# First layer of a four-part transformer kernel: the f16 operand copies move from VectorE to GpSimd

## The chip, the cores and the metric

The kernel runs on one core of one Trainium2 chip. The metric is device microseconds (us) of one execution, the median of several runs. The core has five engines with queues of their own: PE (TensorE, with its weight loads as PEld), DVE (VectorE), ACT (ScalarE), POOL (GpSimd) and SP (SyncE, which only issues DMAs here). They meet only through semaphores.

## What is computed

Eight sequences (B = 8) of 256 tokens with 512 features go through two gated layers. Each adds an attention and a feed-forward part to x:

```python
x = x + tanh(g_xattn[0]) * causal_attention(layernorm(x), ctx, ctx)     # 16 heads of 32, no projections
x = x + tanh(g_ffn[0])   * experts(layernorm(x))                        # 32 experts of 192, 8 per token
x = x + tanh(g_xattn[1]) * projected_attention(layernorm(x), ctx)       # w_q, w_k_img, w_v_img, w_o
x = x + tanh(g_ffn[1])   * ternary_linear(layernorm(x))
```

In the first attention the query is the normalised input, and key and value are both the context. Products need nearly f32 accuracy, so each operand is split into two f16 parts: hi = f16(scale * v), lo = f16(scale * v - hi).

## The kernel before

The program has three stages, each a block with one instruction stream per engine: `layer0` (first attention, gate and sending of rows to expert slots; about the first 330 us), `experts` (160 tiles of 128 rows through the expert weights), and `layer1`. Only `layer0` and, in three lines, `experts` are touched.

**Staging of layer 0.** A batch is one sequence. Its attention has 16 steps (STEPS): 8 for the first half of the queries (keys 0 to 127), 8 for the second half (256 keys), two heads each. In a step PE makes scores (L240, with the causal mask L243), DVE takes their maximum (L325) and scales it to a bias (L327), ACT takes the exponential (L293), PE turns the probabilities (L278), ACT copies them out of PSUM (L305) and PE multiplies them with the context (L258). While batch n runs through its 16 steps, every engine also does the preparation of batch n + 1 (PREP0) and the rest of batch n - 1 (POST0). Which piece is done behind which step is written out by hand in the tables PREP0 and POST0: engine, step number, names of pieces. Within an engine everything runs in that order. Batch 0 has its preparation ahead of the first step, in the order of ORDER_PREP0; the bodies of batches 0 to 6 hold the other seven.

**Preparation pieces.** "ln": DVE takes mean and variance of x (L615, L619, L621), POOL makes the reciprocal root (L605). "c": the two 128-row tiles of the context are split. ACT writes hi (L349), DVE writes lo (L355) and then copies both parts beside themselves in the same `parts` tile (L361), so that each head has four blocks of 32 columns: hi, hi, lo, lo for the context, and hi, lo, hi, lo for the input. "xn": DVE normalises x (L625). "q": the same split and copy for the two tiles of the normalised input. "S0" to "S7": PE turns eight heads of `parts` (L372, eight transposes into one PSUM bank), and DVE (L379), or ACT for S1 and S5 (L318), copies the bank into `stack`, from which the scores are made. S0 and S1 belong to the first context tile, S2 and S3 to the second, S4 to S7 to the two input tiles. PE waits for `parts_ready` ahead of each, and for the copy of the piece two before (the two banks alternate).

The part that copies is this, with the arguments cut; `chain.link` marks an instruction on a semaphore of DVE and waits for it on DVE:

```python
def dve_lo(self, dve, b, i, src, scale, chain):
    j = ORDER[i]
    dve.wait_ge(self.hi_ready, 4 * b.n + i + 1)
    chain.link(scalar_tensor_tensor(self.part(j, 1), src, scale, self.part(j, 0), MULT, SUBTRACT))   # L355
    ...
    self.nc.vector.tensor_copy(dup, of).then_inc(self.parts_ready, 1)                                # L361
```

**POOL in layer 0.** Besides L605 and the second reciprocal root L689 it only issues the indirect DMAs that send the rows of batch n - 1 to their expert slots (L699): 16 per batch, one behind each step (from step 10 of batch n to step 9 of the next body), each behind `probs_made` of its step. In a step, the pieces of the tables stand ahead of the send.

**Rest of a batch on DVE (POST0)** beside the steps of the next: L714 to L726 (division by the sums, gate, variance), L729 (normalised rows, then ACT L681 and L685 and PE L655), L733 (lo part of the rows sent), and the choice of the eight experts (L737 to L782).

**Experts.** For each of the 160 tiles PE loads a code from a table into a register (L1335), turns eight pieces of the tile (L1293), multiplies with gate and up weights (L1305, 12 products), turns the hidden values (L1316) and multiplies with the down weights (L1329). DVE loads a code of its own (L1449). SP loads the block number with bounds (L1157: `min_val=0, max_val=NONE`), the other engines without. `over_tiles` (L1099) writes the first five and last three tiles out, and holds the others in a loop of eight tiles per turn.

**Layer 1** uses the same class Attention with `causal=False`.

Of the kernel before, what the change touches and what calls it, by code (L numbers as in the profile page):

```python
# [14 lines left out]
ALU = mybir.AluOpType  # L15
# [6 lines left out]
QT = S // P  # L22
HC = H // P
NH, D = 16, 32
E, FI, TOPK = 32, 192, 8
# [84 lines left out]
def over_batches(first, body, last):  # L110
# [32 lines left out]
    pool={4: ["ln"]},  # L143
# [47 lines left out]
class Attention:  # L191
# [6 lines left out]
    def __init__(self, nc, sb, sem, bank, tag, causal, scale, v, id32, id16, idb, maskb):  # L198
# [13 lines left out]
        self.hi_ready, self.parts_ready = sem(tag + "hi_ready"), sem(tag + "parts_ready")  # L212
        self.stack_ps, self.stack_ready, self.stack_by_act = sem(tag + "stack_ps"), sem(tag + "stack_ready"), sem(tag + "stack_by_act")
# [138 lines left out]
    def dve_lo(self, dve, b, i, src, scale, chain):  # L352
        j = ORDER[i]
        dve.wait_ge(self.hi_ready, 4 * b.n + i + 1)
        chain.link(self.nc.vector.scalar_tensor_tensor(self.part(j, 1), src.rearrange("p (h d) -> p h d", d=D), scale,  # L355
                                                       self.part(j, 0), ALU.mult, ALU.subtract))
        if j < QT:
            dup, of = self.parts[:, j, :, 1:4:2, :], self.parts[:, j, :, 0:4:2, :]
        else:
            dup, of = self.parts[:, j, :, 2:4, :], self.parts[:, j, :, 0:2, :]  # L360
        self.nc.vector.tensor_copy(dup, of).then_inc(self.parts_ready, 1)  # L361

# [141 lines left out]
def layer0(nc, shared, plan, proj, x, ctx, g_xattn, g_ffn, gate_w, w_experts, mats, ternary):  # L504

    es = ExitStack()
    with es:
# [94 lines left out]
        def pool_prep0(pool, b, piece):  # L602
            if piece == "ln":
                pool.wait_ge(x_var, b.n + 1)
                nc.gpsimd.tensor_tensor(rstd[:, 0, :], mv[:, 0, :, 1], neghalf[:, 0:QT], ALU.pow).then_inc(x_rstd, 1)  # L605

        K_PREP0 = 2 * QT + 2 * QT
# [503 lines left out]
def experts(nc, shared, plan, proj, w_experts, mats, ternary, ctx, vecs):  # L1111

    es = ExitStack()
    with es:
# [4 lines left out]
        def sem(name):  # L1119
            return es.enter_context(nc.semaphore(name))  # L1120
# [161 lines left out]
        def _(pe):  # L1282
# [51 lines left out]
            def step(t):  # L1334
                code = pe.value_load(t_pe[0:1, t.column()])  # L1335
                e, before = code & (E - 1), code >> 5
                if t.at(1).exists():
                    turn(t.at(1))
                gate_up(t, e)
                if t.at(-2).exists():  # L1340
                    turn_h(t.at(-2))
                if t.at(-3).exists():
                    down(t.at(-3), before)
# [59 lines left out]
        def _(dve):  # L1403
# [36 lines left out]
            for t in range(3):  # L1440
                e = dve.value_load(t_e[0:1, t : t + 1])
# [6 lines left out]
            def step(t):  # L1448
                code = dve.value_load(t_dve[0:1, t.column()])  # L1449
# [512 lines left out]
```

## Time and profile before

| what | value |
|---|---|
| median of 3 runs | 1558.1 us (1552.81 to 1558.12) |
| span of the profiled execution (first to last instruction) | 1525.3 us |
| own time of the profiled execution | not stated by the page; the median stands 32.8 us above its span |
| PE / DVE / ACT / POOL busy over the span | 86% / 64% / 60% / 34% |
| mean granted TensorE clock | 0.939 |
| chain that ended last: PE / DMA / DVE / issue / ACT | 45% / 9% / 9% / 8% / 3% |

The shares are averages over three stages with different limits. What the change does has to be read from layer 0, in a batch in mid-flow, and from the loop of tiles in the experts' stage. Start times in all rows are us from the start of the span.

### The profile page before, as it was taken

The numbers are of one execution on the slowest core, as the hardware profiler recorded it, in microseconds if no ns is written. First come the engines' busy times: TensorE is split into PE (matmuls) and PEld (weight loads), VectorE is DVE, ScalarE is ACT, GpSimd is POOL, SyncE is SP. The second block draws the span as 40 slices with busy tenths as digits, with TensorE's granted clock in tenths as the row PEclk, the third lists the DMA queues.
The fourth block names the chain that finished last, engine by engine and source line by source line (L and its number), as shares of the span: only waits on it lengthen the run. The fifth ranks groups of instructions, "written<-read, shape, count | busy, mean of one in ns | idle before, by whom it ended". The sixth has DMA issues, their size and how long they took to land.

```text
span 1525.3 us, 37150 instructions
## 1 busy us (share of the span) xinstructions
PE 1309.4 (86%) x10733; PEld 834.6 (55%) x10734; DVE 972.8 (64%) x2387; ACT 920.1 (60%) x2261; POOL 520.1 (34%) x531
## 2 busy tenths in 40 slices
PE   5888888837999999999999999477989889898984
PEld 3656655524556666665666666144556555555552
DVE  5888888755456665655655633255787777776853
ACT  4777777724556666666666666244766667667661
POOL 1044444455333433332000001665554444541000
PEclk9988888968999999999999999688999999999997
DMA  2044344458888767767676545775654555642000
GB/s 72 29 173 180 146 146 151 156 213 304 269 285 282 256 219 261 238 217 244 218 242 222 181 149 154 126 111 83 98 99 65 104 82 84 100 65 52 15 1 28
DMA packets 96131, 233.39 MB, mean 153 GB/s; under 512 B 11808, under 2 KB 11808, under 8 KB 91424
## 3 DMA queue, kind: packets, MB, share of 16 engines
q0 software_dynamic: 33712, 113.79, 29.8%
q1 hardware_dynamic: 62320, 118.34, 23.3%
q8 instruction: 55, 0.90, 0.3%
q14 instruction: 44, 0.36, 0.1%
HBM read 140.84 MB, written 91.24 MB: 152 GB/s over the span
## 4 chain that ended last, share of the span: by engine, by line
PE 45%; DMA 9%; DVE 9%; issue 8%; ACT 3%; POOL 3%; SPq 1%; DVEq 0%; ACTq 0%; POOLq 0%
PE bank L1305 18%; PE bank L1329 10%; PE bank L1542 6%; DMA xs<-y_tiles,slot_ix 5%; PE bank L1293 4%; PE bank L258 2%; PE bank L1316 1%; PE bank L278 1%; DMA xg<-x_slots 1%; DVE l_nmax L325 1%; PE bank L1548 1%; POOL xs L430 1%; DMA x_slots<-blank 1%; DVE l_stack L379 1%; PE bank L240 1%
## 5 line engine op out<-in xcount | busy, mean ns | idle before, releaser
L1305 PE MATMUL bank<-wh,xT 128*128 x1280 | 343.3, 330 | 4.7 <-DVE hp L1420 4.4
L430 POOL DMA_INDIRECT xs<-y_tiles,slot_ix x120 | 194.6, 1622 | 234.2 <-DMA y_tiles<-ysb 99.1
L293 ACT ACTIVATE l_probs<-bank,l_bias 128x256 f32<-128x256 f32 (+1 forms) x512 | 224.4, 449 | 64.4 <-DVE l_bias L327 64.0
L1305 PE MATMUL bank<-wl,xT 128*128 x640 | 211.4, 330 | 0.0
L325 DVE TENSOR_REDUCE l_nmax<-bank 128x2 f32<-128x512 f32 (+1 forms) x256 | 158.1, 617 | 70.8 <-PE bank L240 41.3
L1410 DVE SCALAR_TENSOR_TENSOR hv<-bank,sg 128x192 f32<-128x192 f32 x160 | 56.9, 356 | 227.5 <-ACT sg L1364 203.5
L1379 ACT ACTIVATE ysb<-bank,xg 128x512 f32<-128x512 f32 x160 | 109.9, 687 | 119.1 <-PE bank L1329 119.1
L305 ACT ACTIVATE l_probsT<-bank 128x512 f32<-128x512 f32 (+1 forms) x256 | 140.0, 547 | 65.6 <-PE bank L278 65.2
L1358 ACT ACTIVATE xT<-bank 128x1024 f16<-128x1024 f16 x160 | 162.5, 1016 | 15.0 <-PE bank L1293 14.8
L1305 PEld LDWEIGHTS bank<-wh,xT 128*128 128x128 f16 x1280 | 126.5, 99 | 81.3 <-issue 11.1
L1329 PE MATMUL bank<-wh,hT 128*128 x480 | 156.1, 380 | 0.9 <-issue 0.9
L240 PE MATMUL bank<-l_stack 128*128 128x256 f16 (+1 forms) x512 | 105.7, 275 | 59.1 <-ACT l_probs L293 49.3
L278 PE MATMUL bank<-id,l_probs 128*128 128x128 f32 x896 | 149.7, 286 | 2.1 <-ACT l_probsT L305 0.5
L699 POOL DMA_INDIRECT x_slots<-room,slot_ix x112 | 113.4, 1013 | 108.3 <-issue 47.0
L1542 PE MATMUL bank<-w_hi,halfT 128*128 128x512 f16 x384 | 125.9, 390 | 18.9 <-DVE accb L1659 17.1
L1200 POOL DMA_DIRECT2D raw<-in_experts_dram x30 | 16.8, 560 | 334.1 <-DVE wl L1436 333.8
L1364 ACT ACTIVATE sg<-bank 128x192 f32<-128x192 f32 x160 | 52.8, 330 | 113.8 <-PE bank L1305 113.8
L1329 PE MATMUL bank<-wl,hT 128*128 x320 | 121.4, 379 | 0.0
L1293 PEld LDWEIGHTS bank<-id,xg 128*128 128x128 f16 x1280 | 84.9, 99 | 58.7 <-DMA xg<-x_slots 22.6
L1293 PE MATMUL bank<-id,xg 128*128 128x128 f16 x1280 | 98.9, 221 | 19.1 <-DMA xg<-x_slots 18.9
L278 PEld LDWEIGHTS bank<-id,l_probs 128*128 128x128 f32 x896 | 102.6, 147 | 11.7 <-ACT l_probsT L305 7.4
L1436 DVE SCALAR_TENSOR_TENSOR wl<-raw,wh x64 | 95.4, 1491 | 20.0 <-issue 15.9
(246 smaller groups left out, 2538.1 us busy)
## 6 DMA issues: line engine op xcount, KB each, us to landing
xg<-x_slots SPq DMA_DIRECT2D x160, 272.0 KB, 2.8
y_tiles<-ysb SPq DMA_DIRECT2D x160, 256.0 KB, 2.5
raw<-in_experts_dram POOLq DMA_DIRECT2D x30, 1280.0 KB, 7.1
x_slots<-blank SPq DMA_DIRECT2D x33, 272.0 KB, 3.6
xs<-in_x_dram SPq DMA_DIRECT2D x8, 512.0 KB, 4.4
cbuf<-in_ctx_dram SPq DMA_DIRECT2D x8, 512.0 KB, 5.8
stage<-in_mats_dram POOLq DMA_DIRECT2D x4, 1024.0 KB, 7.8
room<-in_ctx_dram SPq DMA_DIRECT2D x8, 512.0 KB, 4.6
```

The source lines that it names most:

```text
L240: last = self.nc.tensor.matmul(o, self.stack[:, b.par, 0, h, qt * P : (qt + 1) * P], self.stack[:, b.par, 1, h, 0:nk], start=True, stop=no ...
L278: last = self.nc.tensor.transpose(self.pT[s % len(self.pT)][:, (2 * kt + u) * P : (2 * kt + u + 1) * P], self.probs[:, s % 2, u, kt * P : ...
L293: last = self.nc.scalar.activation(self.probs[:, s % 2, u, 0:nk], self.pS[s % 2][:, u * S : u * S + nk], ACT.Exp, bias=self.bias[:, s % 4, ...
L305: self.nc.scalar.activation(self.probsT[:, s % 2, 0:w], self.pT[s % len(self.pT)][:, 0:w], ACT.Copy).then_inc(self.probsT_made, 1)
L325: self.nc.vector.tensor_reduce(self.nmax[:, s % 4, :], v, AX, ALU.max).then_inc(self.max_made, 1)
L430: return nc.gpsimd.indirect_dma_start(to, None, self.y_tiles[0 : (MT + 1 - k) * P, :], ix, compute_op=ALU.add)
L699: nc.gpsimd.indirect_dma_start(shared.x_slots, bass.IndirectOffsetOnAxis(ap=slot_ix[:, QT * b.n + t, k % TOPK : k % TOPK + 1], axis=0), xe ...
L1293: last = nc.tensor.transpose(o[:, c * P : (c + 1) * P], rows[:, c * P : (c + 1) * P], id16[:])
L1305: last = nc.tensor.matmul(bGU[t.place % 2][:, 0:GU], xT[:, t.place % 2, xo + c * P : xo + (c + 1) * P], wp[:, bass.ds(w, 1), c * GU : (c + ...
L1329: last = nc.tensor.matmul(bY[t.place % 2][:, :], h, wp[:, bass.ds(w, 1), at : at + H].rearrange("p a w -> p (a w)"), start=k == 0, stop=k ...
L1358: nc.scalar.activation(xT[:, t.place % 2, :], bX[t.place % 2][:, :].bitcast(F16), ACT.Copy).then_inc(x_ready, 1)
L1542: last = nc.tensor.matmul(o, xT[:, xo + c * P : xo + (c + 1) * P], w[:, c * H : (c + 1) * H], start=n == 0, stop=n == len(todo) - 1)
```

## The change

In layer 0 (the attention with `causal=True`) DVE no longer copies the parts beside themselves. Its lo instruction counts up a new semaphore, `lo_ready`, and DVE doesn't wait for it. POOL waits for that semaphore and does the copy, which counts up `parts_ready` as before. In the table, POOL has the copies of the context behind "ln" at step 4, and those of the input at step 6, each ahead of that step's send. Layer 1 keeps its copies on DVE. DVE's count of chain marks falls from 8 to 4 per batch. In addition three register loads of the experts' stage, one on PE and two on DVE, are given bounds.

```diff
 PREP0 = dict(
-    pool={4: ["ln"]},
+    pool={4: ["ln", "c"], 6: ["q"]},
@@ Attention
+        if causal:
+            self.lo_ready = sem(tag + "lo_ready")
@@ Attention.dve_lo
         dve.wait_ge(self.hi_ready, 4 * b.n + i + 1)
+        if self.causal:
+            self.nc.vector.scalar_tensor_tensor(self.part(j, 1), src.rearrange("p (h d) -> p h d", d=D), scale,
+                                                self.part(j, 0), ALU.mult, ALU.subtract).then_inc(self.lo_ready, 1)
+            return
@@ Attention
+    def pool_dup(self, pool, b, i):
+        j = ORDER[i]
+        pool.wait_ge(self.lo_ready, 4 * b.n + i + 1)
+        if j < QT:
+            dup, of = self.parts[:, j, :, 1:4:2, :], self.parts[:, j, :, 0:4:2, :]
+        else:
+            dup, of = self.parts[:, j, :, 2:4, :], self.parts[:, j, :, 0:2, :]
+        self.nc.gpsimd.tensor_copy(dup, of).then_inc(self.parts_ready, 1)
@@ pool_prep0
+            else:
+                for t in range(QT):
+                    at.pool_dup(pool, b, t + QT * (piece == "q"))
-        K_PREP0 = 2 * QT + 2 * QT
+        K_PREP0 = 2 * QT
@@ experts
-                code = pe.value_load(t_pe[0:1, t.column()])
+                code = pe.value_load(t_pe[0:1, t.column()], min_val=0, max_val=E * E)
-                e = dve.value_load(t_e[0:1, t : t + 1])
+                e = dve.value_load(t_e[0:1, t : t + 1], min_val=0, max_val=E - 1)
-                code = dve.value_load(t_dve[0:1, t.column()])
+                code = dve.value_load(t_dve[0:1, t.column()], min_val=0, max_val=2**24)
```

DVE in the body of a batch, where the two context tiles are split (the line numbers of the changed file are higher by what was added). Before:

```order
L355 SCALAR_TENSOR_TENSOR l_parts<-cbuf,l_parts 128x16x32 [waits l0_hi_ready,c_loaded0]
L361 COPY l_parts<-l_parts 128x16x64 [waits dve_prep]
L355 SCALAR_TENSOR_TENSOR l_parts<-cbuf,l_parts 128x16x32 [waits l0_hi_ready]
L361 COPY l_parts<-l_parts 128x16x64 [waits dve_prep]
L325 TENSOR_REDUCE l_nmax<-bank 128x2 [waits l0_scores]
L327 TENSOR_SCALAR l_bias<-l_nmax 128x2 [waits l0_max]
L379 COPY l_stack<-bank 128x8x128 [waits l0_stack_ps]
```

And in the changed kernel:

```order
L358 SCALAR_TENSOR_TENSOR l_parts<-cbuf,l_parts 128x16x32 [waits l0_hi_ready,c_loaded0]
L358 SCALAR_TENSOR_TENSOR l_parts<-cbuf,l_parts 128x16x32 [waits l0_hi_ready]
L327 TENSOR_REDUCE l_nmax<-bank 128x2 [waits l0_scores]
L329 TENSOR_SCALAR l_bias<-l_nmax 128x2 [waits l0_max]
L395 COPY l_stack<-bank 128x8x128 [waits l0_stack_ps]
```

Both copies and their waits on DVE's own semaphore are gone; nothing else moved.

POOL in the same body, from the second reciprocal root on. Before:

```order
L689 TENSOR_TENSOR rstd<-mv,neghalf 128x2 [waits p_var]
L699 DMA x_slots<-room,slot_ix 65664x544 [waits l0_probs_s]
L605 TENSOR_TENSOR rstd<-mv,neghalf 128x2 [waits x_var]
L699 DMA x_slots<-room,slot_ix 65664x544 [waits l0_probs_s] x6
L699 DMA x_slots<-room,slot_ix 65664x544 [waits slots_ready,xe_full,l0_probs_s,xe_lo]
```

And in the changed kernel:

```order
L708 TENSOR_TENSOR rstd<-mv,neghalf 128x2 [waits p_var]
L718 DMA x_slots<-room,slot_ix 65664x544 [waits l0_probs_s]
L621 TENSOR_TENSOR rstd<-mv,neghalf 128x2 [waits x_var]
L377 COPY l_parts<-l_parts 128x16x64 [waits l0_lo_ready] x2
L718 DMA x_slots<-room,slot_ix 65664x544 [waits l0_probs_s] x2
L377 COPY l_parts<-l_parts 128x32x32 [waits l0_lo_ready] x2
L718 DMA x_slots<-room,slot_ix 65664x544 [waits l0_probs_s] x4
L718 DMA x_slots<-room,slot_ix 65664x544 [waits slots_ready,xe_full,l0_probs_s,xe_lo]
```

Two copies now stand between the reciprocal root and the next send, two more behind two sends.

PE in the experts' stage, at the load of a tile's code. Before, and then in the changed kernel:

```order
L1335 TENSOR_LOAD t_pe
L1293 MATMUL bank<-id,xg 128x128 [waits x_ready,x_in2]
L1293 MATMUL bank<-id,xg 128x128 x7
L1299 REGISTER_ALU [waits x_ready]
L1299 REGISTER_ALU
```

```order
L1354 TENSOR_LOAD t_pe
L1354 ISA x2
L1312 MATMUL bank<-id,xg 128x128 [waits x_ready,x_in2]
L1312 MATMUL bank<-id,xg 128x128 x7
L1318 REGISTER_ALU [waits x_ready]
```

The bounds put two instructions of the sequencer behind each load, on PE as here and on DVE at its loads.

## Rows read from the trace of the kernel before

**Rows 1.** Table by stretch: busy us and counts, granted clock (PEclk), DMA share, GB/s
```profile
98.00:107.50 9.50, 6.98 (x43) 4.87 (x44) 8.80 (x23) 5.78 (x20) 5.42 (x6) 0.50 0.56 227
108.00:135.00 27.00, 22.98 (x264) 17.08 (x261) 22.29 (x67) 20.56 (x71) 12.19 (x13) 1.00 0.44 159
480.00:540.00 60.00, 60.00 (x465) 37.66 (x463) 38.21 (x97) 37.92 (x66) 25.67 (x33) 1.00 0.78 267
```

**Rows 2.** Timeline of DVE, context pieces: start us, us, what, [idle before it]
```profile
102.92 0.69 DVE L355 SCALAR_TENSOR_TENSOR l_parts<-cbuf,l_parts 128x512 f16<-128x512 f32 x1
103.65 0.43 DVE L361 COPY l_parts<-l_parts 128x1024 f16<-128x1024 f16 x1
103.99 0.68 DVE L355 SCALAR_TENSOR_TENSOR l_parts<-cbuf,l_parts 128x512 f16<-128x512 f32 x1
...
105.82 0.69 DVE L379 COPY l_stack<-bank 128x1024 f16<-128x1024 f16 x1
```

**Rows 3.** Timeline of PE, first context piece and the transposes behind it
```profile
104.75 1.04 PE L372 MATMUL bank<-id,l_parts 128*128 128x128 f16 x8
105.58 1.06 PE L655 MATMUL bank<-id,room 128*128 128x128 f32 x4
```

**Rows 4.** Timeline of POOL, reciprocal root and a send
```profile
103.09 1.10 POOL L605 TENSOR_TENSOR rstd<-mv,neghalf 128x2 f32<-128x2 f32 x1 [1.77 <-DVE mv L621]
...
112.12 0.97 POOL L699 DMA_INDIRECT x_slots<-room,slot_ix  x1 [2.27 <-ACT l_probs L293]
```

**Rows 5.** POOL groups by form: count, busy us, mean ns, idle before
```profile
L1256 POOL CAST w_hi<-stage 128x512 f16<-128x512 f32 x16 | 9.8, 615 | 1.1
...
L1236 POOL CAST slot_f<-slot_ix 128x128 f32<-128x128 int32 x1 | 0.3, 287 | 7.9 <-DMA raw<-in_experts_dram 7.9
```

**Rows 6.** Timeline of DVE, input pieces and what stands behind them
```profile
109.93 0.69 DVE L355 SCALAR_TENSOR_TENSOR l_parts<-room,l_parts 128x512 f16<-128x512 f32 x1
...
112.77 0.31 DVE L327 TENSOR_SCALAR l_bias<-l_nmax 128x2 f32<-128x2 f32 x1
112.85 0.68 DVE L733 SCALAR_TENSOR_TENSOR room<-room 128x512 f16<-128x512 f32 x1
113.45 0.22 DVE L737 COPY lg<-bank 128x64 f32<-128x64 f32 x1
```

**Rows 7.** Timeline of POOL, then of DVE, in the experts' stage
```profile
411.45 0.61 POOL L1256 CAST w_hi<-stage 128x512 f16<-128x512 f32 x1
```
```profile
400.22 0.29 DVE L1419 TENSOR_TENSOR hp<-hv,hp 128x128 f16<-128x128 f32 x1
...
411.54 0.68 DVE L1419 TENSOR_TENSOR hp<-hv,hp 128x128 f16<-128x128 f32 x1
```

**Rows 8.** Timeline of DVE, first context piece of three later batches
```profile
140.29 0.69 DVE L355 SCALAR_TENSOR_TENSOR l_parts<-cbuf,l_parts 128x512 f16<-128x512 f32 x1
...
215.24 0.69 DVE L355 SCALAR_TENSOR_TENSOR l_parts<-cbuf,l_parts 128x512 f16<-128x512 f32 x1
...
252.77 0.69 DVE L355 SCALAR_TENSOR_TENSOR l_parts<-cbuf,l_parts 128x512 f16<-128x512 f32 x1
```

**Rows 9.** Timeline of PE, preparation of batch 0
```profile
11.28 2.90 PE L372 MATMUL bank<-id,l_parts 128*128 128x128 f16 x24 [11.28 <-DVE l_parts L361]
...
17.20 2.92 PE L372 MATMUL bank<-id,l_parts 128*128 128x128 f16 x24 [1.84 <-DVE l_parts L361]
```

**Rows 10.** L1157 on SP: count, ns min/median/max, first and last start
```profile
L1157 SPq FUSED_REGOPS  x280: 46/152/162, 342.1 to 939.2; - x140
...
L1157 SPq SEQ_ASSERT  x160: 18/18/18, 342.3 to 939.4; - x160
```

**Rows 11.** L1335 in 497 to 498 us, then PEld's timeline
```profile
L1335 PEldq TENSOR_LOAD <-t_pe x1: 537/537/537, 496.6 to 496.6; - x1
```
```profile
498.28 0.65 PEld L1293 LDWEIGHTS bank<-id,xg 128*128 128x128 f16 x8
...
502.00 0.57 PEld L1293 LDWEIGHTS bank<-id,xg 128*128 128x128 f16 x8 [0.19 <-issue]
```

## The prediction, written before the changed kernel was run

> **What bounds the kernel now.** I read the table by stretch first, since the page's shares mix three stages. In the experts' stage PE is busy 60.00 of 60 us at full clock [rows 1]: there only what delays PE counts. Layer 0 is another matter. In 98 to 107.5 us, part of the body of one batch, DVE is busy 8.80 of 9.50 us and PE's granted clock is 0.50, that is 1.2 GHz; in 108 to 135 us the clock is 1.00 (2.4 GHz) and no engine is full (PE 22.98 of 27, DVE 22.29) [rows 1]. So a batch has a stretch where DVE leads and, inside it, a stretch where PE works at the low clock. I then read the timelines of the engines around the copies, because the question is which of the four copies of a batch somebody waits for.
>
> *The context copies.* DVE makes lo at 102.92, copies at 103.65, makes the second lo at 103.99 [rows 2]. PE begins S0 at 104.75 with no idle time shown before it, is through at 105.79, and the transposes of L655 begin behind it at 105.58 [rows 3]. DVE's copy of S0 out of PSUM starts at 105.82, just when PE is done [rows 2]. So DVE here ends up waiting for PE: time saved on DVE just before S0 buys nothing.
>
> *The input copies.* From 109.93 to 113.45 DVE has no idle time at all: lo, copy, lo, copy, maximum, bias, L733, L737 [rows 6]. Here DVE leads, and a shorter DVE is an earlier bias.
>
> **The change part by part.**
>
> 1. *What DVE saves.* One lo and its copy take 103.99 - 102.92 = 1.07 us from start to start [rows 2]. An instruction of the same kind with no wait on its own result behind it takes 113.45 - 112.85 = 0.60 us [rows 6]. So a copy is worth 0.47 us of DVE. Two of the four copies of a batch lie where DVE leads: -0.94 us per batch. The other two, also 0.94 us, only make it wait longer for S0.
>
> 2. *What a copy costs on POOL.* No row shows this copy (1024 f16 per partition). The nearest are casts: 615 ns for 512 elements, 287 ns for 128 [rows 5]. That is 0.18 us fixed and 0.85 ns per element, so an estimated 1.05 us for 1024. Bounds: 0.61 us if 16-bit pairs move as one element, 1.23 us for twice the cast. I take 1.05, since both casts are one-input moves as this one is. The Trainium skill ("GPSIMD Engine Reference", section "Engine selection") calls one-input work on GpSimd roughly line-rate, and its section "Performance versus the Vector engine" gives 1.03 cycles per element at 1.2 GHz for the lightest bodies. Its estimate would be 0.88 us plus a start-up, and the wait in step 3 would be 0.48 instead of 0.65 us; no run here shows it yet.
>
> 3. *S0 becomes late.* POOL's reciprocal root L605 runs from 103.09 to 104.19 [rows 4], and the copy stands behind it. With some 0.1 us between instructions it runs 104.3 to 105.4. PE wanted the parts at 104.75 [rows 3]: PE waits 0.65 us, and with it L655, ACT behind that, and DVE's S0 copy. Bounds: 0.2 us with the 0.61 us copy, 0.95 us if the copy takes 1.23 us and the root comes out 0.1 later. The second context tile (copied till 106.5) isn't wanted before S2, after the transposes of L655, so it costs nothing.
>
> 4. *DVE and POOL hold each other up.* In the experts' stage a POOL cast ran 411.45 to 412.06, and the DVE subtraction that started at 411.54 took 0.68 instead of the 0.29 us of its like at 400.22 [rows 7]: it ended just after the cast did. In layer 0 the bias at 112.77 took 0.31 us beside a send that began at 112.12 [rows 6, 4]; most take 0.17. The Trainium skill ("SBUF — State Buffer", section "Who interferes with whom") calls this an exclusive lock on a shared port pair, taken by whichever starts first, for a DVE instruction with two SBUF inputs or in a two-port mode. By that rule the removed DVE copy was itself a holder, and the new POOL copy is one for more than twice as long; the rows just named agree. For the two input copies POOL is busy about 2.1 us, from the end of the first lo on. In it fall the maximum (its input is in PSUM, so I let it pass), the bias, L733 and the small selections. The bias loses up to 0.4 us, L733 nothing if it starts first or about 1.0 if POOL's second copy does. So 0.4 to 1.4, and I take 0.9 per batch, the middle, since nothing says who starts first. Zero is the lower bound if short operands don't collide.
>
> 5. *A batch summed*: -0.94 + 0.65 + 0.9 = +0.6 us. Bounds -0.7 (-0.94 + 0.2 + 0) and +1.4 (-0.94 + 0.95 + 1.4).
>
> 6. *Batch 0* has no steps to hide in: PE waits for the copies at 11.28 and at 17.20 [rows 9]. POOL's root ends there at about 11.25 as well, so the first copy ends 1.1 us later than PE began. The second wait gets the difference of the copies once more (1.05 + 0.1 - 0.43 = 0.7). Together +1.8 us.
>
> 7. *What becomes of a shift.* The first context piece starts at 102.92, 140.29, 215.24 and 252.77 [rows 2, 8]. The distances are 37.37, twice 37.48, and 37.53 us: they close in on a value just above 37.5. I read this as follows. The low-clock stretch [rows 1] ends at a time that doesn't move when a batch moves a little. PE's run of S0, L655 and S1 lies in it. A batch that comes 1 us later has 1 us less of the half-speed stretch, so it gives about half of the delay back, and an earlier batch loses half of its gain. With 7 x 0.6 + 1.8 = +6.0 us put in, and half given back each batch, the end of layer 0 moves by about 0.6/0.5 = +1.2 us. That is my term; the term without feedback is +6.0.
>
> 8. *Moved sends.* The sends of steps 4 to 9 start some 2 to 4 us later. POOL was idle 2.27 us before the one at 112.12 [rows 4], so they have caught up before step 10, and their rows are wanted a batch later. Nothing.
>
> 9. *The bounds on register loads.* On SP, where the load has bounds already, they show as a register instruction of 152 ns and an assert of 18 ns per load [rows 10]; with the gaps around them I take 0.25 us of sequencer time. On a common tile PE's load ends at 497.14 and its first weight load of L1293 comes at 498.28 [rows 11]: the sequencer is 1.1 us ahead, and 0.25 disappears. At the loop's turn PEld stood idle 0.19 us for issue, at 502.00 [rows 11]; there it counts in full. Of the 160 tiles 19 are such turns, so at most 19 x 0.25 = 4.8 us. Most turns have some lead; I take +2 us. On DVE the same two instructions fall into its wait for ACT: nothing, or a few tenths.
>
> **Sum**: +1.2 + 2 = +3.2 us. The span would go from 1525.3 to 1528.5. The page gives no time of its own for the profiled execution; the 32.8 us between its span and the median of 1558.1 I take as unchanged. Forecast 1561.3 us. A measurement of this kernel can tell from no change about 0.5%, or 7.8 us, so this is no change.
>
> **The rivals.**
>
> *A. The delay is kept* (slower). POOL holds S0 up in every batch, the lock costs its upper bound and there is no feedback: 7 x 1.4 + 1.8 + 2 to 4.8 = +13.6 to +16.4, about 1573 us. For it: PE takes S0 without a pause now, and the copy gets more than twice as long. Against it: the distances in rows 8. It decides from the point where PE's wait before S0 is over 0.7 us and the distance of the batches leaves 37.5.
>
> *B. DVE is what counts* (faster). POOL's copies are in time, they block nothing, and all of the 1.88 us of DVE per batch come back: -13.2 + 1.8 + 2 = -9.4, or 1548.7 us. For it: DVE is busy 8.80 of 9.50 us in the low-clock stretch [rows 1]. Against it: its S0 copy waits for PE there, and the feedback would keep only a fraction.
>
> *C. PE's sequencer isn't ahead.* If each of the 160 tiles paid the 0.25 us: +40 us, or about 1598. The lead of 1.1 us [rows 11] speaks against it; for it, only that a shortage once begun may take several tiles to fill up.
>
> **How the numbers follow.** Forecast 0.66, A 0.20, B 0.11, C 0.03. The forecast's own values run from -0.7/0.5 + 0 = -1.4 to +6.0 + 4.8 = +10.8, though its upper end needs both extremes. The range from 1552 to 1570 holds all of that, leaves out most of A, B and C, and allows for runs that differ by 5.3 us among themselves. Faster by over 0.5% (under 1550.3) is most of B: 0.09. Slower by over 0.5% (over 1565.9) is A, C and little of the forecast: 0.22. The rest, 0.69, is within.
>
> **What would show each step.** On POOL: 32 copies of about 1.05 us; under 0.7 or over 1.3 and step 2 is wrong. On PE: idle time before the S0 transposes in the body, released by POOL, of about 0.65 us. On DVE: the bias and L733 behind the input pieces longer than 0.17 and 0.68 us (step 4). The first context pieces still about 37.5 us apart (step 7); at 36.5 or 39 that step has failed, and with it the forecast. In the experts' stage common tiles as far apart as before, and more idle time for issue before L1293 at the turns (step 9).

## The result, and the profile after

| | before | after |
|---|---|---|
| median of the runs on this chip | 1558.01 us (4 runs, 1552.81 to 1558.12) | 1570.06 us (4 runs, 1568.86 to 1576.59) |
| ratio, with its 95% interval | | 1.0092 [1.0069, 1.0116] |
| span of the profiled execution | 1525.3 us | 1567.1 us |

The changed kernel is slower, by 12 us between the medians, and the whole interval lies above the 0.5% that can be told from no change. The forecast was +3.2 us and the range ended at 1570. The spans differ by 41.8 us, over three times as much as the times do: that is the first thing to explain. The profiled execution of after took 1568.86 us, 1.8 us more than its span.

The page of after:

```profile
span 1567.1 us, 37796 instructions
...
PE 1316.8 (84%) x10733; PEld 837.0 (53%) x10734; DVE 967.0 (62%) x2355; ACT 924.1 (59%) x2261; POOL 556.2 (35%) x563
```

Only 32 instructions went from DVE to POOL. Now the places the prediction named. POOL's timeline of after, a batch in the middle of layer 0 (start us, us, what, idle before it); it answers to [rows 4]:

```profile
108.27 1.10 POOL L621 TENSOR_TENSOR rstd<-mv,neghalf 128x2 f32<-128x2 f32 x1 [1.76 <-DVE mv L640]
109.35 2.01 POOL L377 COPY l_parts<-l_parts 128x1024 f16<-128x1024 f16 x2
...
116.14 2.95 POOL L377 COPY l_parts<-l_parts 128x1024 f16<-128x1024 f16 x2 [2.04 <-DVE l_parts L358]
```

PE's timeline of after, the first stack transposes S0 and those behind them [rows 3]:

```profile
110.43 1.03 PE L388 MATMUL bank<-id,l_parts 128*128 128x128 f16 x8 [0.43 <-POOL l_parts L377]
111.25 1.06 PE L674 MATMUL bank<-id,room 128*128 128x128 f32 x4
```

DVE's timeline of after in the same batch [rows 2, 6]:

```profile
108.11 1.29 DVE L358 SCALAR_TENSOR_TENSOR l_parts<-cbuf,l_parts 128x512 f16<-128x512 f32 x2
...
109.77 0.63 DVE L329 TENSOR_SCALAR l_bias<-l_nmax 128x2 f32<-128x2 f32 x1
111.50 0.69 DVE L395 COPY l_stack<-bank 128x1024 f16<-128x1024 f16 x1 [1.10 <-PE bank L388]
...
117.32 0.28 DVE L329 TENSOR_SCALAR l_bias<-l_nmax 128x2 f32<-128x2 f32 x1
```

The context copies take 1.0 us each, the input copies 1.48. PE now waits 0.43 us for POOL's first copy, where it waited for nothing, and DVE has 1.10 us of idle time before its S0 copy: the DVE time that was saved stands there as a wait. The bias beside the context copies took 0.63 us against the usual 0.17; the one beside the input copies took 0.28.

Batch 0 in PE's timeline of after [rows 9]:

```profile
12.13 2.90 PE L388 MATMUL bank<-id,l_parts 128*128 128x128 f16 x24 [12.13 <-POOL l_parts L377]
...
19.09 2.92 PE L388 MATMUL bank<-id,l_parts 128*128 128x128 f16 x24 [2.89 <-POOL l_parts L377]
```

Against 11.28 and 17.20 it is 1.9 us late by the second wait. So far everything is near what was forecast. What was not is the distance of the batches. DVE's timeline of after, the first context piece of later batches [rows 8]:

```profile
151.52 0.69 DVE L358 SCALAR_TENSOR_TENSOR l_parts<-cbuf,l_parts 128x512 f16<-128x512 f32 x1
...
195.24 0.69 DVE L358 SCALAR_TENSOR_TENSOR l_parts<-cbuf,l_parts 128x512 f16<-128x512 f32 x1
...
239.19 0.69 DVE L358 SCALAR_TENSOR_TENSOR l_parts<-cbuf,l_parts 128x512 f16<-128x512 f32 x1
```

They are 43.4 us (from 108.11), 43.72 and 43.95 us apart instead of 37.5. Part of the 6 us more is idle time of a kind that the trace of before doesn't have at all: waits that the view puts down to "remote", because it finds no instruction of this core whose signal ended them. The timeline of all engines of after, where the idle time of 133 us lies:

```profile
132.32 0.22 PE L245 MATMUL bank<-maskb,idb 128*128 128x128 bf16 x1
...
132.38 0.61 PE L280 MATMUL bank<-id,l_probs 128*128 128x128 f32 x4
132.55 0.97 POOL L718 DMA_INDIRECT x_slots<-room,slot_ix  x1 [0.42 <-issue]
134.37 0.69 DVE L327 TENSOR_REDUCE l_nmax<-bank 128x2 f32<-128x512 f32 x1 [2.93 <-remote]
134.43 0.60 ACT L307 ACTIVATE l_probsT<-bank 128x512 f32<-128x512 f32 x1 [2.68 <-PE bank L280]
135.07 0.37 PEld L260 LDWEIGHTS bank<-l_probsT,cbuf 128*32 128x32 f32 x8 [2.33 <-ACT l_probsT L307]
```

By the profile PE was through with the scores at 132.54 and with the transposes of L280 at 132.99. DVE, which waits for the first, and ACT, which waits for the second, both start at 134.4. That is 1.4 to 1.8 us after the ends that the profile gives for PE, which are modelled. Three of the "remote" waits of after in 100 to 340 us (engine, line, waited for: us in total, times, longest):

```profile
DVE l_nmax L327 <- remote: 11.8, 4, 3.0
DVE att L735 <- remote: 5.0, 2, 2.5
DVE slot L791 <- remote: 4.0, 4, 1.0
```

With a fourth row of 1.5 us DVE's come to 22.3 us in these 240, or some 4 us per batch; ACT has 3.6 us of them. So they are a part of what the batches grew by, not all of it.

The experts' stage seems unchanged: from the first to the last of the 160 tile loads it took 603.4 us before and 603.8 after. But that is one execution each, and the experiments show how far they scatter.

### The profile page after: what moved, and what is told of

The parts are those of the page before. It is cut to its first block, busy times and chain, and to the rows that moved or that the text cites. A ratio compares the mean times of both kernels' runs of the same rounds, so it can differ in the third digit from the quotient of the medians.

```text
span 1567.1 us, 37796 instructions
## 1 busy us (share of the span) xinstructions
PE 1316.8 (84%) x10733; PEld 837.0 (53%) x10734; DVE 967.0 (62%) x2355; ACT 924.1 (59%) x2261; POOL 556.2 (35%) x563
## 4 chain that ended last, share of the span: by engine, by line
PE 39%; issue 9%; DMA 9%; DVE 8%; ACT 4%; POOL 3%; SPq 2%; DVEq 1%; ACTq 0%; POOLq 0%
PE bank L1324 16%; PE bank L1348 8%; PE bank L1561 5%; DMA xs<-y_tiles,slot_ix 5%; PE bank L1312 3%; POOL xs L446 2%; PE bank L260 2%; DMA xg<-x_slots 1%; PE bank L280 1%; DMA x_slots<-blank 1%; PE bank L1335 1%; DVE l_nmax L327 1%; PE bank L1567 1%; ACT l_probs L295 1%; PE bank L242 1%
## 5 line engine op out<-in xcount | busy, mean ns | idle before, releaser
L327 DVE TENSOR_REDUCE l_nmax<-bank 128x2 f32<-128x512 f32 (+1 forms) x256 | 158.3, 618 | 88.7 <-PE bank L242 41.2
L280 PE MATMUL bank<-id,l_probs 128*128 128x128 f32 x896 | 150.1, 286 | 2.3 <-ACT l_probsT L307 0.5
L280 PEld LDWEIGHTS bank<-id,l_probs 128*128 128x128 f32 x896 | 103.2, 147 | 12.2 <-ACT l_probsT L307 7.7
```

The source lines that it names most:

```text
L280: last = self.nc.tensor.transpose(self.pT[s % len(self.pT)][:, (2 * kt + u) * P : (2 * kt + u + 1) * P], self.probs[:, s % 2, u, kt * P : ...
L327: self.nc.vector.tensor_reduce(self.nmax[:, s % 4, :], v, AX, ALU.max).then_inc(self.max_made, 1)
```

## The experiments

Three questions: do the "remote" idles belong to the change, what do the bounds cost, what do the copies cost. The chip differs from one group of four experiments to the next, so ratios are compared, or kernels of one group. The forecasts in us were made for a chip on which the kernel before takes 1558 us, and have to be read as ratios or differences elsewhere. The kernel before took 1521.98 us on the chip of E1 to E4, 1522.67 on that of E5 to E8, and 1555.88 on that of E9 to E12.

**E1, the bounds alone.** The kernel before with these lines of the change and nothing else:

```
-                code = pe.value_load(t_pe[0:1, t.column()])
+                code = pe.value_load(t_pe[0:1, t.column()], min_val=0, max_val=E * E)
-                e = dve.value_load(t_e[0:1, t : t + 1])
+                e = dve.value_load(t_e[0:1, t : t + 1], min_val=0, max_val=E - 1)
-                code = dve.value_load(t_dve[0:1, t.column()])
+                code = dve.value_load(t_dve[0:1, t.column()], min_val=0, max_val=2**24)
```

> The kernel before with the three bounds on register loads and nothing else of the change. Theory S (the cost is the copies on POOL): the bounds cost at most 1 us, so 1558 to 1559 us; no DVE idle put down to 'remote' of 2 us or more in layer 0, and batches about 37.5 us apart. Theory B (the bounds cost): the experts' stage grows by 2 to 5 us and the whole is 1560 to 1563. Theory P (the profiled execution of before, with a span of 1525.3 us, was not what a usual execution is): this kernel's profiled span is near 1556 us, its layer 0 is some 30 us longer than that of before's trace, and the same 'remote' idles stand in it, since they come with the sends and not with the copies.

Measured: 1529.27 us against 1521.98, ratio 1.0047 [1.0024, 1.0071]. Theory S is wrong about the bounds: they cost 7 us, with 4 to 11 inside the interval. Theory B had the right place, and its 2 to 5 us lie at the low end of that. Theory P is wrong in its numbers: its span was 1526.9 us, near that of before's trace, and it has no "remote" idle. But P asked the right question: this chip runs the old kernel in 1522 us, not in 1558. Before's profiled execution, 1525.3 plus about 1.8 us, fits such a chip; then it was never 32.8 us shorter than its own time. Its chip isn't on record, so this is inferred from the span and from layer 0.

**E2, the change without TensorE's bound.**

```
-                code = pe.value_load(t_pe[0:1, t.column()], min_val=0, max_val=E * E)
+                code = pe.value_load(t_pe[0:1, t.column()])
```

> The changed kernel without the bound on TensorE's register load. Theory S: 1569 to 1570 us, as the change, since the first expert load and the last one are as far apart as before. Theory B: 2 to 4 us less than the change, 1566 to 1568.

Measured: 1529.17 us, ratio 1.0047 [1.0030, 1.0063]. As a ratio it is 0.0017 under the change itself (E5), which is the direction of theory B, within the uncertainty of both. Theory S would have had 1.0070 or more, above the interval.

**E3 and E4, half of the copies.** E3 has the context copies on POOL and the input copies on DVE, E4 the reverse:

```
-    pool={4: ["ln", "c"], 6: ["q"]},
+    pool={4: ["ln", "c"]},
...
-        if self.causal:
+        if self.causal and i in (0, 1):
...
```

> Only the context copies are on POOL, the input copies back on DVE. Theory S in its first form (the start of each batch is late, because the first stack transposes wait for a POOL copy of 1.0 us and DVE is held by it): most of the 12 us stays, 1567 to 1570 us. Theory Q (the cost is in the input copies, which at 1.48 us each are longer than the context copies and stand close ahead of the sends on POOL's queue): most goes, 1559 to 1562 us.

> Only the input copies are on POOL, the context copies back on DVE. Theory S in its first form: 1558 to 1561 us. Theory Q: 1567 to 1570 us. If both halves cost about the same, e3 and e4 are each near 1564.

Measured: E3 1534.32 us, ratio 1.0088 [1.0054, 1.0122]; E4 1534.78 us, ratio 1.0081 [1.0051, 1.0111]. Neither theory has both. Over E1 it is 5 us each, and the two don't add up to the whole: E5, with both, came to 1.0064. With intervals of 0.003 to either side the times leave the split open. The traces say more: the loads of the 160 tiles in the experts' stage (ns min/median/max, first and last start), of E3 and then of E4:

```profile
L1354 PEldq TENSOR_LOAD <-t_pe x160: 297/531/1151, 350.4 to 955.3; - x160
```

```profile
L1354 PEldq TENSOR_LOAD <-t_pe x160: 297/530/1452, 345.7 to 957.4; - x160
```

In the four traces of chips of 1522 us whose layer 0 is that of before (before, E1, E6, E7) the first load starts at 343.5 to 345.7 us. With the context copies on POOL it is at 350.4, clearly later; with the input copies alone at 345.7, no later. So by these traces it is the context copies that cost in layer 0. What E4 is longer by lies in the experts' stage, 611.7 us, the longest of all traces, where no copy was moved: how much of its 5 us belongs to the copies isn't shown.

**E5, the change again; E6, DVE's two bounds without TensorE's.** E6 is E1 less the first pair of lines.

> The change itself once more. Theory T (two parts that add up: bound on TensorE's register load some 5 us by bubbles in the experts' stage, copies on POOL some 4 to 6 us in layer 0): ratio 1.006 to 1.010 on any chip, and on a chip on which the kernel before takes about 1522 us the batches of layer 0 are 37.6 to 38.2 us apart, not 44. Theory U (the POOL copies bring the 'remote' idles of 2.5 to 3 us with them): 44 us apart wherever it runs, and 40 us more than before on a fast chip.

> The kernel before with the two bounds on DVE's register loads and without the one on TensorE's. Theory T: within 0.1 per cent of before, ratio 1.000 to 1.002, since e1's 7 us are TensorE's. If DVE's bounds are the ones that cost, the ratio is 1.004 to 1.005 as in e1.

Measured: E5 1531.51 us against 1522.67, ratio 1.0064 [1.0045, 1.0084]; E6 1525.28 us, ratio 1.0016 [0.9998, 1.0034]. Theory U falls: here the change has no "remote" idle. Theory T's ratio for E5 came true, but its batches, 37.6 to 38.2 us apart, did not in this trace; E6 is inside the 1.000 to 1.002 in the median, not within the 0.1% that was also said, and its interval, up to 1.0034, overlaps that of E1. DVE's timeline of E5, the first context pieces:

```profile
178.73 0.69 DVE L358 SCALAR_TENSOR_TENSOR l_parts<-cbuf,l_parts 128x512 f16<-128x512 f32 x1
...
216.17 0.69 DVE L358 SCALAR_TENSOR_TENSOR l_parts<-cbuf,l_parts 128x512 f16<-128x512 f32 x1
...
253.59 0.69 DVE L358 SCALAR_TENSOR_TENSOR l_parts<-cbuf,l_parts 128x512 f16<-128x512 f32 x1
```

The distances are 37.44 and 37.42 us, as before the change [rows 8]. E2, whose layer 0 is the same program, has 38.00, 37.89, 37.73 and 37.65 in its trace, so 37.4 is not the whole picture. Within a batch that of after returns to the hundredth: S0 waits 0.43 us for POOL, DVE 1.10 us for S0. So some 6 of the 43.9 us per batch in the trace of after appear only on a chip of the slower kind. The table by stretch of two batches (from, to, length, busy us of PE, PEld, DVE, ACT, POOL, granted clock, DMA share, GB/s), of E5 and then of E1:

```profile
139.00:213.60 74.60, 59.61 (x616) 43.93 (x616) 62.09 (x173) 54.70 (x186) 45.87 (x45) 0.89 0.43 156
```

```profile
139.00:213.60 74.60, 60.77 (x616) 44.73 (x616) 63.75 (x182) 54.43 (x188) 36.20 (x36) 0.87 0.41 149
```

DVE is 0.83 us per batch less busy, POOL 4.8 us more, and the batch is about as long as it was. PE's granted clock is 0.89 here and 0.87 in E1. Over the last four distances between the batches' first context pieces it is 0.89 in E5 and 0.86 in E2, so the shorter batches of E5 go with the higher clock.

**E7, a second bound on TensorE.** E1 with one more register operation (38 ns in the median) and assertion (18 ns) per tile:

```
                 code = pe.value_load(t_pe[0:1, t.column()], min_val=0, max_val=E * E)
+                code = nc.s_assert_within(code, 0, E * E - 1)
```

> The kernel of e1 with a second bound on the same value on TensorE, so that each tile has its register operation and assertion twice. Theory T (after a register load TensorE's sequencer has only as much time as the matmuls already issued last, and each piece added behind the load comes out as a bubble where the load is long): over e1 again 5 to 15 us, ratio to before 1.008 to 1.014. If what costs in e1 is something else (the experts' stage differing by chance between runs), the ratio stays at 1.004 to 1.005.

Measured: 1532.17 us, ratio 1.0081 [1.0055, 1.0106]. That is 0.0034 or 5 us over E1, the low end of what theory T gave. The times alone don't separate it from E1, since the intervals overlap; the waits do. One row each of PEld's waits in the experts' stage (us in total, times, longest), for the transposes that come straight behind the register load, first of before, then of E6, E1 and E7:

```profile
PEld bank L1293 <- issue: 1.8, 5, 0.5
```

```profile
PEld bank L1293 <- issue: 2.8, 9, 0.4
```

```profile
PEld bank L1293 <- issue: 7.9, 19, 0.9
```

```profile
PEld bank L1293 <- issue: 22.2, 56, 1.2
```

Without TensorE's bound PEld stands idle there 5 times (before) and 9 times (E6, E2; 10 in E10) in 160 tiles, with one bound 19 times (17 to 25 in the seven such traces), with two 56 times. The same row of after:

```profile
PEld bank L1312 <- issue: 8.9, 25, 0.8
```

What the bound added, in the view by line of after's L1354 (count, ns min/median/max, first and last start) [rows 10, 11], and below it the load's row in the trace of before:

```profile
L1354 PEldq FUSED_REGOPS  x293: 42/151/165, 386.8 to 990.6; - x147
L1354 PEldq TENSOR_LOAD <-t_pe x160: 297/494/1248, 386.2 to 990.0; - x160
L1354 PEldq SEQ_ASSERT  x160: 18/18/28, 387.0 to 990.8; - x160
```

```profile
L1335 PEldq TENSOR_LOAD <-t_pe x160: 297/308/1375, 345.7 to 949.1; - x160
```

Before has 133 of the register operations, of 42 ns each; the 160 that were added take 151 ns. Besides, the load itself lasts longer in the median, 494 ns instead of 308.

The length of the stage, from the first of these loads to the last, scatters by more than the effect, so one pair of traces (603.4 and 603.8 us) shows nothing. Over all traces of this study it does: four without TensorE's bound (before, E2, E6, E10) took 597 to 603 us, 600.7 in the mean; seven with it straight behind the load (after, E1, E3, E4, E5, E8, E12) 602 to 612, 606.1 in the mean; E7 611.1. Of these 5.4 us about half is time in which PE isn't busy (15.9 us in the mean without, 18.5 with). The rest stands as longer PE records (584.8 and 587.6 us in sum), so the idles of PEld are a sign of the cost and not its whole account.

The tile in [rows 11], with its load of 537 ns and lead of 1.1 us, was far from the longest load, 1375 ns. Behind the long ones nothing is left of the lead: in E1 six of the seven loads of over 0.9 us have an idle of PEld of more than 0.2 us behind them, and of the other 153 only three.

**E8, each POOL copy twice.** The change with the copy made again after the first:

```
+            self.dup_once = sem(tag + "dup_once")
...
-        self.nc.gpsimd.tensor_copy(dup, of).then_inc(self.parts_ready, 1)
+        self.nc.gpsimd.tensor_copy(dup, of).then_inc(self.dup_once, 1)
+        pool.wait_ge(self.dup_once, 4 * b.n + i + 1)
+        self.nc.gpsimd.tensor_copy(dup, of).then_inc(self.parts_ready, 1)
```

> The change with each of the four POOL copies of a batch made twice, the second waiting for the first. The copies are on the path (the first stack transposes wait for them): each doubled context copy of 1.0 us delays the start of a batch by 1 to 2 us, eight batches, so 8 to 20 us over the change, ratio to before 1.012 to 1.02. If they are off it, within 3 us of the change.

Measured: 1546.36 us, ratio 1.0149 [1.0127, 1.0172], 13 us over the change by the ratios and 15 between the medians. The copies are on the path. S0 in PE's timeline of E8:

```profile
153.98 1.03 PE L391 MATMUL bank<-id,l_parts 128*128 128x128 f16 x8 [1.53 <-POOL l_parts L380]
```

It waits 1.53 instead of 0.43 us, and from the third batch on the distances are 39.0 to 39.6 us, to the last. A delay that is put in here stays in.

**E9, TensorE's bound behind the transposes.** E1 with the bound moved:

```
-                code = pe.value_load(t_pe[0:1, t.column()], min_val=0, max_val=E * E)
-                e, before = code & (E - 1), code >> 5
+                code = pe.value_load(t_pe[0:1, t.column()])
                 if t.at(1).exists():
                     turn(t.at(1))
+                code = nc.s_assert_within(code, 0, E * E)
+                e, before = code & (E - 1), code >> 5
```

> The kernel of e1 with the bound on TensorE's value put behind the eight transposes of the next tile's rows instead of straight behind the load; the load stays where it was. Theory T (the 0.25 us of the bound count because they lie between the load and the next matmul): the eight transposes are issued before the bound, but they last 0.45 us in all against the 0.25 us, so the loss is much smaller than in e1: ratio 1.001 to 1.003 against 1.0047. Rival V (the bound costs wherever it stands, because TensorE's sequencer, not its matmuls, sets the pace of a tile): 1.004 to 1.005 as in e1.

Measured: 1565.48 us against 1555.88, ratio 1.0053 [1.0034, 1.0071]. Nothing was won: the 1.001 to 1.003 of theory T lie outside the interval. PEld's wait for issue before L1293 fell to 3.4 us, 7 times, but idle time appears behind the bound's new place. The row of the groups by line, PE in the experts' stage, first of E1, then of E9:

```profile
L1305 PE MATMUL bank<-wh,xT 128*128 x1267 | 338.1, 329 | 6.8 <-DVE hp L1420 5.7 <-issue 0.6
```

```profile
L1305 PE MATMUL bank<-wh,xT 128*128 x1267 | 339.0, 330 | 9.2 <-DVE hp L1421 4.6 <-issue 4.0
```

E11, with the bound in the same place, has 5.1 us for issue in that row, and the seven traces with the bound straight behind the load have 0.2 to 1.0. Rival V is right about the time, and the bubble has moved. That TensorE's sequencer sets the pace of every tile, V's reason, is not shown; the stage took 606.5 us here and 601.8 in E11, which doesn't place the cost any closer.

E9's chip is one of 1556 us, and its layer 0 is that of the kernel before. Its "remote" waits in 100 to 340 us:

```profile
ACT l_probsT L305 <- remote: 8.3, 6, 2.7
DVE l_stack L379 <- remote: 7.7, 5, 2.1
DVE att L716 <- remote: 7.1, 3, 2.5
```

So the "remote" idles are there without the change too, though at other instructions, and from the third batch on the distances are 39.8, 42.3, 40.5, 43.3 and 41.5 us. The experts' first transposes start at 376.39 us here and at 343.99 in E1 with the same layer 0: 32.4 us, which is what the prediction had called the gap between span and median.

**E10, three copies on POOL, without TensorE's bound.** The first context copy, for which S0 waits, is back on DVE:

```
-        if self.causal:
+        if self.causal and i > 0:
...
-                for t in range(QT):
+                for t in range(piece == "c", QT):
                     at.pool_dup(pool, b, t + QT * (piece == "q"))
```

> The change without TensorE's bound and with the first context copy of a batch, the one that the first stack transposes wait for, back on DVE; the other three stay on POOL. If the wait of these transposes for POOL's first copy is what the copies cost, the start of a batch is no longer late: first expert load at 344 to 347 us instead of 348 to 350, ratio 1.000 to 1.003. If the cost is DVE held by POOL's copies, nothing is won over e2: 1.004 to 1.006.

Measured: 1566.15 us, ratio 1.0060 [1.0036, 1.0083]. The interval leaves out the 1.000 to 1.003 that were expected if S0's wait were the cost, and holds the 1.004 to 1.006 of the other reading; but these were counted for chips of 1522 us. In the trace the first load of the experts' stage starts at 378.0 us, against 376.4 in E9 and 384.9 and 385.9 in E12 and E11, which would speak for a gain. But that execution was the shortest of the seven (1557.18 us), 9 us under the median. Whether taking S0 off POOL gains anything stays open.

**E11 and E12, the change with E9's bound, and the change itself.**

> The whole change with TensorE's bound behind the transposes as in e9. Theory T: less than the change by what e9 is less than e1, ratio 1.003 to 1.005. Rival V: as the change, 1.006 to 1.009.

> The change a third time, beside e9 and e11 on one chip. Ratio 1.006 to 1.010. Should the kernel before take 1558 us on this chip: 'remote' idles in the trace of e9 too, whose layer 0 is that of before, and its batches 43 to 44 us apart, so that they belong to the chip and not to the change; on a chip of 1522 us none in either.

Measured: E11 1572.23 us, ratio 1.0098 [1.0069, 1.0127] (one of its six runs took 5439 us, unexplained; without it the median is 1571.52); E12 1569.87 us, ratio 1.0098 [1.0071, 1.0126]. Rival V again. Compared with E9 on the same chip, the copies cost 0.0045 or 7 us, with an uncertainty of some 4 to 5 us. PE's timeline at the start of the experts' stage, of E9 and of E12, shows it in layer 0:

```profile
376.39 2.18 PE L1293 MATMUL bank<-id,xg 128*128 128x128 f16 x16 [8.32 <-DMA xg<-x_slots]
```

```profile
384.92 1.03 PE L1312 MATMUL bank<-id,xg 128*128 128x128 f16 x8 [8.39 <-DMA xg<-x_slots]
```

Layer 0 ends 8.5 us later. On the chips of 1522 us the same row of E1 and of E5 reads

```profile
343.99 1.03 PE L1293 MATMUL bank<-id,xg 128*128 128x128 f16 x8 [7.41 <-DMA xg<-x_slots]
```

```profile
347.93 2.17 PE L1312 MATMUL bank<-id,xg 128*128 128x128 f16 x16 [8.82 <-DMA xg<-x_slots]
```

and the difference is 3.9 us. In E2, with the same layer 0 as E5, the first load starts at 349.6 us. The four traces with the layer 0 of before have it at 344.5 us in the mean, so E5 is 3.4 and E2 5.1 us later. No variant was faster than the kernel before.

## Why the prediction was wrong, step by step

The sign was right and the size was not: +3.2 us forecast, 12 us measured. Two terms of the sum were too small, the shift of layer 0 (+1.2 us, steps 7 and 8) and the bounds (+2 us, step 9), and the comparison of spans hid both.

- **What DVE saves (step 1).** 0.47 us per copy, from start to start, was forecast, or 1.88 us for the four of a batch. DVE's busy time fell by 0.83 us per batch in E5, under half of that; how much of the rest is overlap in the records and how much is DVE held up in exchange isn't separated. Where it was saved before S0, it became the 1.10 us wait, as said.
- **The copy on POOL (step 2).** 1.05 us forecast, 1.03 measured for one copy alone; 1.0 and 1.48 us in the two pairs. The Trainium skill ("GPSIMD Engine Reference", section "Performance versus the Vector engine") led to 0.88 us plus a start-up. The measured 1.03 us leaves 0.15 us for that, and the two casts' 0.85 ns per element [rows 5] is near the 0.86 that is estimated from that section's cycles, so the traces agree.
- **S0 late (step 3).** 0.65 us forecast, 0.43 measured. Right in kind.
- **Who holds whom (step 4).** The 0.9 us were placed on DVE beside the input copies. There the bias lost only 0.11 us and POOL lost 0.45 us per copy; DVE's second lo and what follows had started first. Beside the context copies the bias did lose 0.46 us, under cover of the wait for S0. The Trainium skill ("SBUF — State Buffer", section "Who interferes with whom") has it that the order of issue decides who is blocked, and these rows agree: that POOL can be the one that is held is the half that the step had left out of its number.
- **Batch sum and batch 0 (steps 5, 6).** Batch 0 came out at +1.9 us against 1.8. The last four distances are 37.37 us on average in the four traces of the faster kind with the layer 0 of before, 37.42 in E5 and 37.82 in E2: 0.05 and 0.45 us more, inside the bounds of -0.7 to +1.4 and under the 0.6.
- **The feedback (step 7): the first failing term.** It took the +6.0 us of layer 0 down to +1.2, because half of every delay was to be given back. On the chips of 1522 us the start of the experts' stage moved by 3.4 and 5.1 us (E5 and E2), so most of it was kept. E8 shows it plainly: it puts more delay into every batch, and the distances stay at 39.0 to 39.6 us instead of returning to 37.5. Distances that settle at a constant value show a steady pace; they don't say what a delay would do to it. A weaker return isn't excluded: E2's distances fall from 38.00 to 37.65 us, and the small batch term of E5 goes with a higher granted clock.
- **Moved sends (step 8).** Forecast at nothing. From E1 to E5 the first context piece of the last batch moved by 2.6 us (250.99 to 253.59), and the first expert tile by 3.9: 1.3 us were added behind the last batch, where the experts' first load waits for the sends (8.82 us of idle time instead of 7.41). The forecast had followed a send in the body only, not the last ones.
- **The bounds (step 9): the second failing term, and the larger one.** +2 us forecast, +7 measured (E1; its interval allows 4 to 11). The step took the 0.25 us to be hidden on common tiles because one tile had 1.1 us of lead, and let only the 19 turns of the loop pay. The loads of before vary between 0.3 and 1.4 us; the ordinary lead doesn't cover the long ones, and 5 to 10 idles became 17 to 25. The row that was read was one of 160. The minimum, median and maximum of the same line in the trace of before would have said so. Rival C, at +40 us, had the mechanism with the wrong weight: the shortage comes at some tiles, not at all 160. Of DVE's bounds, costed at nothing, E6 can't exclude 0 to 5 us.
- **The 32.8 us between span and median.** They were "taken as unchanged", with no reason. By E1 and E9 they are the difference between two kinds of chip. The times were to be measured on one of 1558 us. There the copies cost 7 us (E12 over E9), on chips of 1522 us 2.6 us (E5 over E1) or 4.7 (E2 over E6), each with 4 to 5 us of uncertainty: the times don't show that they cost more on the slower chips. The traces hint at it, with 8.5 us in layer 0 (E12 over E9) against 3.4 and 5.1. No row of before could show the idles that make up the difference between such chips; but 32.8 us without a row was a sign that the trace was of another situation, and the range should have been wider for it.

The sum in hindsight: bounds 7, copies 3 to 5 (chips of 1522 us) or 7 (chips of 1556), so 10 to 12 or 14 us. Measured: 9, 12 and 14 us between the medians in E5, the result and E12. Rival A was nearest in time with 13.6 to 16.4 us. It had half of the mechanism, that the delay is kept; but about half of the cost lies in the experts' stage, which it left at 2 to 4.8 us, and its 1.4 us per batch show on no chip of 1522 us.

What stays open is whether the copies cost more on the slower chips, and if so, why. In E12 the "remote" idles fall on the maxima of the scores (L327, 10.5 us in four waits), which the softmax waits for; in E9 on the stack copies, the outputs and ACT's copies. In sum they are even smaller in E12, 16.0 us against 23.1. That the copies, by moving the sends, moved the idles to a worse place is a reading of two traces and wasn't tried by itself.

## What to carry to other kernels

When an instruction stream has a lead over its engine, read the spread of what eats the lead, not one instance: a quarter of a microsecond added behind a load of 0.3 to 1.4 us cost 5 to 7 us over 160 tiles, and moving it behind the next eight transposes did not help. Work given to a slower engine pays only where nobody waits for it; here the time that DVE saved before S0 turned into a wait for the first copy. And compare the profiled span with the measured time before anything else: if they don't fit, the trace is of another situation, here most likely another chip, and a difference of spans is no result.

## What the runs showed of the hardware

- Chips differ by 2% on this program: the kernel before took 1522 us on two chips and 1556 us on a third. Its mean granted clock was 0.940 and 0.930 there, so the slower chip also had a little less clock. In the traces at hand the difference lies in layer 0, where the batches of before's program are 37.2 to 37.5 us apart (before, E1, E6, E7) against 39.8 to 43.3 (E9), from the third on. It is not idle time alone: over four batches PE was busy 120.8 us at clock 0.88 in E1 and 129.9 us at 0.83 in E9. Which of the two comes first isn't shown.
- On the slower chips what waits for PE at times starts 1 to 2 us after the end that the profile gives for PE's work, several engines at once. The case shown for 134.4 us lies in layer 0, right behind five sends that POOL issued 1.3 to 1.4 us apart (127.19 to 132.55). The same sends stand in the traces of the faster chips without such idles, and whether they have a part in it was not tried. The Trainium skill ("Perfetto Trace Analysis", section "Per-engine timelines") says that PE's end is an estimate and that its signal goes out after the results are written: so whether the work or the signal was late can't be told, and no run here shows it.
- The register load on PE's queue took 308 to 310 ns in the median of the four traces without TensorE's bound and 464 to 542 ns with the bound straight behind it; it was 505 and 492 in E9 and E11, where the bound stood further on. The prediction took its length as given, and how much of the 7 us comes by the longer load wasn't tried.
